# Scattering token rows behind both normalisations of a unit, with one instruction order for every unit of a streamed attention kernel

## The chip, the cores and the metric

The program runs on one core of a Trainium2 chip. The metric is the device time of one execution in microseconds (us), of which the median of several executions is taken. One more execution of the kernel was recorded by the hardware profiler, and all rows below are from that one. PE is TensorE, DVE is VectorE, ACT is ScalarE, POOL is GpSimd and SP is SyncE, which here only issues DMAs.

## The reference, cut to what matters

```
x  = L0_attn_x                                  # 16 x 512 x 256, float32
xn = layernorm(x)
# attention, 16 heads of 64, causal
q, k, v = xn @ Wq, xn @ Wk, xn @ Wv             # per head
wei = softmax(where(causal, q @ k.T * 64**-0.5, -inf))
att = concat_heads(wei @ v) @ Wo + bo
# experts: 16 experts of width 128, two chosen per token by sigmoid(xn @ gate_w + gate_b)
shared = (silu(xn @ swg) * (xn @ swu)) @ swd
routed = sum over the two chosen experts of value * (silu(xn @ wg[e]) * (xn @ wu[e])) @ wd[e]
out = x + att + (xn + shared + routed)
```

## The kernel before, in words

A first stage (some 100 us) normalises the tokens, stores the normalised rows in DRAM, computes the gate values and splits the weights in a high and a low part. Then one long stream runs through 128 **units**. Unit u is one pair of heads of one batch of 512 tokens: batch u // 8, pair u % 8. A **step** of the stream is one turn of the loop `for u in STEPS`, and each engine has its own copy of that loop with its own order of work.

In step u PE does the following, each part with a letter and line of the profile:

- the transposes of unit u's normalised probabilities in three fills, **t3**, **t1** and **t20** (the fill's number names the blocks of 128 query rows that it holds; 16, 8 and 16 transposes, L690);
- the scores of unit u + 1 in three fills, **s3**, **s1** and **s20** (L701);
- the projections k, v and q of unit u + 2 (L663, L676), the output projection of a finished pair (L731, with L736 in two units of a batch), in one unit of a batch the shared gate and up projections (L747), in another the transposes of the next batch's tokens (L758);
- the product of probabilities and v, L715, with which the step ends.

t3, t1 and t20 of unit u wait for POOL. POOL multiplies the exponentials by the inverse sums (`normalise`, L1314) in two groups of four instructions: the **first normalisation** (blocks 3 and 1) and the **second normalisation** (blocks 2 and 0). In step u POOL normalises unit u + 1. The first group waits for the inverse that DVE writes behind its eight row minima (L986, L992), the second for a later inverse. t3 and t1 need the first group, t20 the second.

POOL has other work in the same queue. In steps with u % 8 of 6, 7, 0 and 1 it adds two things to the running sum of a batch between the two normalisations (`prepare`, L1266 and L1268). In steps 12 to 43 it issues the **scatter** (`scatter`, L1277): each batch's normalised rows go to the places of their two experts in a DRAM table, eight indirect DMAs per batch, four per step. In steps 48 to about 88 it issues gathers of expert weights, and from about step 91 gathers of results, two or more per item (L1305), all behind the second normalisation.

In scatter steps two of the four DMAs stand ahead of the second normalisation and two behind it. There the order of PE and DVE also differs from that of the other steps:

```
def turns_first(u):
    return u < FIRST_SCATTER or u > FIRST_SCATTER + 2 * B
```

FIRST_SCATTER is 12 and B is 16, so the function is false for u from 12 to 44, which is 33 units. Where it is true, PE runs t3, t1, t20, s3, s1, s20. Where it is false, PE runs t3, t1, s3, s1, t20, s20, so that t20 comes later. DVE copies half of every transposed fill out of PSUM (`take_probs`, L979) and follows the same choice: t20's copy stands ahead of the first row minima or between them. ACT's order is the same in both cases. PSUM is a ring of eight banks that the function `order` hands out in PE's order.

In odd steps from 15 to 45, DVE also splits one expert's weights (`split_pack`, L1153, both inputs in SBUF) behind the second inverse.

Of the kernel before, what the change touches and what calls it, by code (L numbers as in the profile page):

```python
# [30 lines left out]
B, T, D = 16, 512, 256  # L31
# [23 lines left out]
FIRST_SCATTER = 12  # L55
# [247 lines left out]
def stream(nc, ins, dram, keep, out):  # L303

    with ExitStack() as ctx:
# [106 lines left out]
        SCATTER_AT = {FIRST_SCATTER + n: (n // 2, n % 2) for n in range(2 * B)}  # L412
# [19 lines left out]
        def half(r):  # L432
            return slice(r * DK, (r + 1) * DK)
# [17 lines left out]
                return {}  # L451
            return {kind: n - back for kind, back in (("dn", 2), ("gu", 1), ("xt", 0)) if 0 <= n - back < SLOT_TILES}

        def turns_first(u):

            return u < FIRST_SCATTER or u > FIRST_SCATTER + 2 * B

        def order(u):

            rows_part = ["t20", "t20", "s3", "s3", "s1", "s1"] if turns_first(u) else ["s3", "s3", "s1", "s1", "t20", "t20"]  # L460
            kinds = ["t3", "t3", "t1", "t1", *rows_part, "s20", "s20", 0, "k", "v", "gate", "q",
                     "o", "up", "sum0", "sum1", "rank0", "rank1", "n0", "n1", 1, "w"]
            for n, kind in enumerate(kinds):
                if kind in (0, 1):
                    for each, t in tick(u, kind).items():
                        yield each, 0, t
                elif there(kind, u):
                    yield kind, int(n > 0 and kinds[n - 1] == kind), u
# [27 lines left out]
        with nc.Block() as block:  # L496
# [153 lines left out]
            def _(pe):  # L650
# [30 lines left out]
                def transposes(fill, u):  # L681
                    to = [take(f"t{fill}", u, r) for r in range(2)]
                    pe.wait_ge(norm_done, 8 * u + NTH[PARTS[fill][-1][0], 1] + 1)
                    slots = sum(i + 1 for i, _ in PARTS[fill])
                    for i, at in PARTS[fill]:
                        for h in range(2):
                            for j in range(i + 1):
                                for r in range(2):
                                    off = (h * slots + at + j) * DK
                                    last = pe.transpose(to[r][:, off:off + DK].bitcast(F32R),  # L690
                                                        moved[half(r), i, h, j * P:(j + 1) * P], ident[half(r), half(r)])
                    last.then_inc(t_ready, 1)
# [119 lines left out]
                for u in STEPS:  # L812
                    attends = 0 <= u < UNITS
                    if attends:
                        transposes(3, u)
                        transposes(1, u)
                    if attends and turns_first(u):
                        transposes(20, u)
                    if there("s3", u):
                        scores(3, u)  # L820
                        scores(1, u)
                    if attends and not turns_first(u):
                        transposes(20, u)
                    if there("s20", u):
                        scores(20, u)
                    ticks(u, 0)
                    if there("k", u):
                        project("k", u)
                        project_v(u)
                    if there("gate", u):  # L830
                        expand("gate", u)
                    if there("q", u):
                        project("q", u)
                    if there("o", u):
                        project_out(u)
                    if there("up", u):
                        expand("up", u)
                    if there("sum0", u):
                        count("sum", u)
                    if there("rank0", u):  # L840
                        count("rank", u)
                    if there("n0", u):
                        turn(u)
                    ticks(u, 1)
                    if attends:
                        weigh(u)
# [128 lines left out]
            def _(dve):  # L975
# [216 lines left out]
                for u in STEPS:  # L1192
                    attends, ahead = 0 <= u < UNITS, there("s3", u)
                    if 0 <= u - 1 < UNITS:
                        split_out(u - 1)
                    if attends:
                        take_probs(3, u)
                        take_probs(1, u)
                    if attends and turns_first(u):
                        take_probs(20, u)  # L1200
                    if ahead:
                        maximum(3, 0, u)
                        maximum(3, 1, u)
                    if attends and not turns_first(u):
                        take_probs(20, u)
                    if ahead:
                        maximum(1, 0, u)
                        maximum(1, 1, u)
                        maximum(2, 0, u)
                        maximum(2, 1, u)  # L1210
                        maximum(0, 0, u)
                        maximum(0, 1, u)
                        invert(31, u + 1)
                    route(u, 0)
                    n = tick(u, 0)
                    if "gu" in n:
                        slot_gate(n["gu"])
                        slot_widen(n["gu"])
                    if "xt" in n:
                        split_xt(n["xt"])  # L1220
                    if there("k", u):
                        split_projected("k", u)
                    if "gu" in n:
                        split_slots(n["gu"])
                    if there("v", u) and u % 2:
                        take_v(u)
                    if there("gate", u):
                        gate(u)
                    if there("q", u):
                        split_projected("q", u)  # L1230
                    if ahead:
                        invert(20, u + 1)
                    if there("o", u):
                        add_out(u)
                    if there("up", u):
                        widen(u)
                    if u in PACK_AT:
                        split_pack(PACK_AT[u])
                    if there("n0", u):
                        split_normal(u)  # L1240
                    done = [m for m, item in enumerate(ITEMS) if item[0] == u - 1]
                    n = tick(u, 1)
                    if "gu" in n:
                        slot_gate(n["gu"])
                        slot_widen(n["gu"])
                    if "xt" in n:
                        split_xt(n["xt"])
                    if there("up", u):
                        split_hidden(u)
                    if "gu" in n:  # L1250
                        split_slots(n["gu"])
                    for part in range(2):
                        for m in done:
                            add_routed(m, part)
                    route(u, 1)

            @block.gpsimd
            def _(pool):
# [68 lines left out]
                for u in STEPS:  # L1327
                    b, k = (u + 2) // PAIRS, (u + 2) % PAIRS
                    if there("s3", u):
                        for i in (3, 1):  # L1330
                            for h in range(2):
                                normalise(i, h, u + 1)
                    if 0 <= b < B and k < QT:
                        prepare(b, k)
                    n = TICKS.get((u, 0))
                    if n is not None and 1 <= n and n + 1 < SLOT_TILES:
                        gather_weights(n + 1)
                    if u == FIRST_TICK - 1:
                        for t in range(2):
                            gather_weights(t)  # L1340
                    if u in SCATTER_AT:
                        scatter(*SCATTER_AT[u], 0)
                    if there("s20", u):
                        for i in (2, 0):
                            for h in range(2):
                                normalise(i, h, u + 1)
                    n = TICKS.get((u, 1))
                    if n is not None and 1 <= n and n + 1 < SLOT_TILES:
                        gather_weights(n + 1)
                    if u in SCATTER_AT:  # L1350
                        scatter(*SCATTER_AT[u], 1)
                    for m, item in enumerate(ITEMS):
                        if item[0] == u:
                            gather_rows(m)
# [49 lines left out]
```

## Time and profile before

| | |
|---|---|
| median of 3 executions | 1960.73 us (1960.04 to 1964.51) |
| the profiled execution's own time | 1962.58 us |
| its span from the first to the last instruction | 1960.9 us |
| mean granted TensorE clock | 0.989 of full speed |
| busy: PE, DVE, ACT, POOL | 1892.3, 1406.0, 1218.2, 1020.2 us |
| units 12 to 44 in the trace (first transpose of unit 12 to that of unit 45) | 282.34 to 706.87 us |

The time of an execution is a little longer than its span. A unit is found in the trace by its first transposes, which follow the previous unit's L715. PE's time in a unit can be read as a **head**, from the first transpose to the first matmul behind the scores, and a rest.

### The profile page before, as it was taken

What the parts mean: (1) busy time and instruction counts of PE and PEld (TensorE: products, weight loads), DVE (VectorE), ACT (ScalarE), POOL (GpSimd) and SP (SyncE); (2) the same over time, 40 slices, a digit from 0 to 9 for tenths busy, and PEclk for the clock granted to TensorE, in tenths of its full rate; (3) what the DMA queues carried; (4) which work ended last, traced back from release to release, by engine and by line L of the source; (5) the groups of instructions that cost most, each with busy time, mean ns of one, the idle gap of its engine ahead of it and who ended that gap; (6) DMA issues with size and microseconds to landing.
All of it is one profiled execution on the core that took longest, in us unless ns stands there. A gap on an engine that the chain in (4) does not pass through costs nothing.

```text
span 1960.9 us, 53515 instructions
## 1 busy us (share of the span) xinstructions
PE 1892.3 (97%) x20556; PEld 1748.2 (89%) x20558; DVE 1406.0 (72%) x4086; ACT 1218.2 (62%) x3340; POOL 1020.2 (52%) x1512
## 2 busy tenths in 40 slices
PE   5879999999999999999999999999999999999998
PEld 5868898888889898999999999999999999888897
DVE  7658886767676676666766667667667888878875
ACT  3355566666666565666665666666666666656564
POOL 2133447777776644344343343344344867687742
PEclk9999999999999999999999999999999999999999
DMA  8534422434343312544545445545432232333200
GB/s 246 192 109 175 153 94 82 138 106 146 109 146 109 114 68 71 194 153 148 175 157 178 147 154 167 171 162 173 147 103 77 87 119 87 114 95 120 70 29 12
DMA packets 158603, 249.92 MB, mean 127 GB/s; under 512 B 27280, under 2 KB 112528, under 8 KB 158352
## 3 DMA queue, kind: packets, MB, share of 16 engines
q1 hardware_dynamic: 134688, 150.79, 23.4%
q0 software_dynamic: 23664, 95.70, 14.8%
q8 instruction: 167, 2.74, 0.6%
q14 instruction: 84, 0.69, 0.1%
HBM read 151.54 MB, written 94.90 MB: 126 GB/s over the span
## 4 chain that ended last, share of the span: by engine, by line
PE 65%; POOL 16%; issue 8%; DVE 3%; ACT 3%; DMA 0%; POOLq 0%; SPq 0%; DVEq 0%
PE d_bank L663 13%; PE d_bank L715 10%; POOL d_probs L1314 9%; PE d_bank L701 9%; PE d_bank L690 8%; PE d_bank L731 6%; PE d_bank L676 6%; PE d_bank L789 6%; POOL queued_rows L1277 4%; PE d_bank L776 3%; ACT d_probs L860 2%; PE d_bank L747 2%; DVE d_probs L986 1%; POOL d_rows L1305 1%; PE d_bank L799 1%
## 5 line engine op out<-in xcount | busy, mean ns | idle before, releaser
L1314 POOL TENSOR_SCALAR d_probs<-d_probs,d_inverse 128x512 f32<-128x512 f32 (+3 forms) x1024 | 554.7, 556 | 756.6 <-DVE d_inverse L992 755.3
L860 ACT ACTIVATE d_probs<-d_probs,d_bias 128x512 f32<-128x512 f32 (+3 forms) x1024 | 562.4, 553 | 119.4 <-DVE d_bias L986 119.4
L986 DVE CUSTOM_DVE_ANT_0 d_probs<-d_bank,mask 128x512 f32<-128x512 f32 (+3 forms) x1024 | 432.5, 484 | 3.2 <-PE d_bank L701 2.5
L663 PE MATMUL d_bank<-d_xnt,wqk_all 128*128 128x512 f32 x1536 | 414.0, 405 | 1.5 <-DVE d_xnt L1039 1.5
L663 PEld LDWEIGHTS d_bank<-d_xnt,wqk_all 128*128 128x128 f32 x1536 | 274.6, 191 | 54.9 <-DVE d_xnt L1039 1.7
L715 PE MATMUL d_bank<-d_probs_t,d_v 128*64 128x128 f32 x5120 | 308.9, 276 | 0.0
L701 PE MATMUL d_bank<-d_ks,d_qs 64*128 64x512 f32 (+3 forms) x3072 | 290.5, 332 | 8.3 <-issue 6.9
L715 PEld LDWEIGHTS d_bank<-d_probs_t,d_v 128*64 128x64 f32 x5120 | 278.1, 137 | 17.1 <-issue 5.4
L701 PEld LDWEIGHTS d_bank<-d_ks,d_qs 64*128 64x128 f32 x3072 | 251.8, 191 | 24.3 <-issue 7.7
L690 PEld LDWEIGHTS d_bank<-ident_r,d_probs_moved 64*128 64x128 f32 x5120 | 226.1, 136 | 48.5 <-issue 48.2
L690 PE MATMUL d_bank<-ident_r,d_probs_moved 64*128 64x64 f32 x5120 | 244.1, 245 | 22.8 <-POOL d_probs L1314 22.0
L853 ACT ACTIVATE d_probs_t<-d_bank 128x512 f32<-128x512 f32 (+1 forms) x384 | 188.2, 525 | 102.1 <-PE d_bank L690 91.9
L997 DVE TENSOR_TENSOR d_qs<-d_bank,d_qs 128x512 fp32r<-128x512 f32 x128 | 88.5, 691 | 201.6 <-ACT d_qs L866 201.6
L878 ACT ACTIVATE d_out_t<-d_bank 128x512 fp32r<-128x512 f32 x128 | 76.4, 597 | 249.5 <-PE d_bank L715 249.5
L979 DVE COPY d_probs_t<-d_bank 128x512 f32<-128x512 f32 (+1 forms) x384 | 209.1, 591 | 8.4 <-PE d_bank L690 7.9
L731 PEld LDWEIGHTS d_bank<-wo_all,d_out_t 128*128 128x128 f32 x1536 | 201.1, 190 | 12.2 <-issue 1.7
L676 PEld LDWEIGHTS d_bank<-wv_all,d_xnt 128*128 128x128 f32 x1536 | 199.4, 190 | 11.1
L731 PE MATMUL d_bank<-wo_all,d_out_t 128*128 128x256 f32 x1536 | 206.7, 281 | 1.5 <-DVE d_out_t L1008 1.5
L676 PE MATMUL d_bank<-wv_all,d_xnt 128*128 128x256 f32 x1536 | 201.2, 281 | 0.0
L860 ACT ACTIVATION_READ_ACCUMULATOR d_probs<-d_probs,d_bias 128x1 f32 x1024 | 194.8, 190 | 0.0
L1008 DVE TENSOR_TENSOR d_out_t<-d_bank,d_out_t 128x512 fp32r<-128x512 f32 x128 | 88.2, 689 | 111.6 <-ACT d_out_t L878 110.7
L1305 POOL DMA_INDIRECT d_rows<-routed_rows,slot x128 | 132.1, 1032 | 34.6 <-issue 34.6
(122 smaller groups left out, 2292.6 us busy)
## 6 DMA issues: line engine op xcount, KB each, us to landing
queued_rows<-d_zeros SPq DMA_DIRECT2D x79, 256.0 KB, 2.4
d_x<-queued_rows SPq DMA_DIRECT2D x79, 256.0 KB, 3.4
routed_rows<-d_y SPq DMA_DIRECT2D x79, 256.0 KB, 2.3
expert_rows<-d_w SPq DMA_DIRECT2D x32, 384.0 KB
a_x_in<-in_L_attn_x SPq DMA_DIRECT2D x16, 512.0 KB, 7.5
xn_rows<-a_xn SPq DMA_DIRECT2D x16, 512.0 KB, 5.2
d_normal<-xn_rows SPq DMA_DIRECT2D x32, 256.0 KB, 3.7
d_base<-in_L_attn_x SPq DMA_DIRECT2D x32, 256.0 KB, 2.9
```

The lines of the kernel that those rows point to most:

```text
L663: last = pe.matmul(to[:, :], wqk[:, n % PAIRS, "qk".index(kind), wa, k, :], xnt[n // PAIRS % 2][:, xb, k, :], start=first, stop=(k == KD - ...
L676: last = pe.matmul(to[:, t * 2 * P:(t + 1) * 2 * P], xnt[b % 2][:, xa, k, tok * P:(tok + 1) * P], wv[:, wb, k, cols], start=(k == 0 and (x ...
L690: last = pe.transpose(to[r][:, off:off + DK].bitcast(F32R), moved[half(r), i, h, j * P:(j + 1) * P], ident[half(r), half(r)])
L701: last = pe.matmul(to[h][:, at * P:at * P + cols], qs[r][qa][half(h), i * P:(i + 1) * P], ks[r][kb][half(h), 0:cols], start=(n == 0), stop ...
L715: last = pe.matmul(to[half(h), i * P:(i + 1) * P], v[u // 2 % 2][:, j, col:col + DK], probs_t[fill][:, h, at + j, :], start=(j == 0), stop ...
L731: last = pe.matmul(to[:, s * D:(s + 1) * D], out_t[g % 2][oa][:, j, cols], wo[:, wb, g % 4 * GROUP + j, :], start=(j == 0 and n == 0), sto ...
L853: act.activation(probs_t[fill][:, :, :, half(0)], bank(f"t{fill}", u)[:, 0:2 * slots * DK].rearrange("p (h j n) -> p h j n", h=2, n=DK), A ...
L860: act.activation(part, part, ACT.Exp, bias=bias[:, i, h:h + 1], scale=-1.0, accum_out=total[which][:, at % 4:at % 4 + 1]).then_inc(exp_don ...
L979: dve.tensor_copy(probs_t[fill][:, :, :, half(1)], bank(f"t{fill}", u, 1)[:, 0:2 * slots * DK].rearrange("p (h j n) -> p h j n", h=2, n=DK ...
L986: dve.tensor_tensor_reduce(out=probs[:, i, h, 0:cols], in0=bank(f"s{fill}", u, h)[:, at * P:at * P + cols], in1=mask[:, T - cols:T], scale ...
L1305: pool.indirect_dma_start(out=rows[m % 4 // 2][:, m % 2 * 2 + n, :], out_offset=None, in_=dram["routed"][:, :], in_offset=bass.IndirectOff ...
L1314: pool.tensor_scalar(part, part, inverse[which][:, at % 4:at % 4 + 1], 1.0, ALU.mult, ALU.mult).then_inc(norm_done, 1)
```

## The change

All four scatter DMAs of a step are issued behind the second normalisation, and `turns_first` is gone: every unit takes the order t3, t1, t20, s3, s1, s20 on PE, with DVE's copy of t20 ahead of the row minima. The numbers of instructions and DMAs don't change.

```diff
-        def turns_first(u):
-
-            return u < FIRST_SCATTER or u > FIRST_SCATTER + 2 * B
-
         def order(u):
 
-            rows_part = ["t20", "t20", "s3", "s3", "s1", "s1"] if turns_first(u) else ["s3", "s3", "s1", "s1", "t20", "t20"]
+            rows_part = ["t20", "t20", "s3", "s3", "s1", "s1"]
...
                     if attends:
                         transposes(3, u)
                         transposes(1, u)
-                    if attends and turns_first(u):
+                    if attends:
                         transposes(20, u)
                     if there("s3", u):
                         scores(3, u)
                         scores(1, u)
-                    if attends and not turns_first(u):
-                        transposes(20, u)
                     if there("s20", u):
                         scores(20, u)
...
                     if attends:
                         take_probs(3, u)
                         take_probs(1, u)
-                    if attends and turns_first(u):
+                    if attends:
                         take_probs(20, u)
                     if ahead:
                         maximum(3, 0, u)
                         maximum(3, 1, u)
-                    if attends and not turns_first(u):
-                        take_probs(20, u)
                     if ahead:
                         maximum(1, 0, u)
                         maximum(1, 1, u)
...
-                    if u in SCATTER_AT:
-                        scatter(*SCATTER_AT[u], 0)
                     if there("s20", u):
                         for i in (2, 0):
                             for h in range(2):
...
                     if u in SCATTER_AT:
-                        scatter(*SCATTER_AT[u], 1)
+                        for half_of in range(2):
+                            scatter(*SCATTER_AT[u], half_of)
```

**POOL, the third scatter step (step 14, where `prepare` runs too).** d_base and d_normal are the running sum, d_probs the probabilities, queued_rows the DRAM table. Before:

```order
L1314 TENSOR_SCALAR d_probs<-d_probs,d_inverse 128x512 [waits d_inverse_done] x2
L1314 TENSOR_SCALAR d_probs<-d_probs,d_inverse 128x256 [waits d_inverse_done] x2
L1266 TENSOR_TENSOR d_base<-d_base,d_normal 128x256
L1268 TENSOR_TENSOR d_base<-d_base,d_bo 128x256 [waits d_x_summed]
L1277 DMA queued_rows<-d_rows_994,slot 20224x256 [waits d_rows_loaded1]
L1277 DMA queued_rows<-d_rows_994,slot 20224x256
L1314 TENSOR_SCALAR d_probs<-d_probs,d_inverse 128x384 [waits d_inverse_done] x2
L1314 TENSOR_SCALAR d_probs<-d_probs,d_inverse 128x128 [waits d_inverse_done] x2
L1277 DMA queued_rows<-d_rows_994,slot 20224x256 [waits d_rows_loaded1]
L1277 DMA queued_rows<-d_rows_994,slot 20224x256
```

After:

```order
L1306 TENSOR_SCALAR d_probs<-d_probs,d_inverse 128x512 [waits d_inverse_done] x2
L1306 TENSOR_SCALAR d_probs<-d_probs,d_inverse 128x256 [waits d_inverse_done] x2
L1258 TENSOR_TENSOR d_base<-d_base,d_normal 128x256
L1260 TENSOR_TENSOR d_base<-d_base,d_bo 128x256 [waits d_x_summed]
L1306 TENSOR_SCALAR d_probs<-d_probs,d_inverse 128x384 [waits d_inverse_done] x2
L1306 TENSOR_SCALAR d_probs<-d_probs,d_inverse 128x128 [waits d_inverse_done] x2
L1269 DMA queued_rows<-d_rows_994,slot 20224x256 [waits d_rows_loaded1]
L1269 DMA queued_rows<-d_rows_994,slot 20224x256
L1269 DMA queued_rows<-d_rows_994,slot 20224x256 [waits d_rows_loaded1]
L1269 DMA queued_rows<-d_rows_994,slot 20224x256
```

The second normalisation (the rows with 384 and 128 columns) has moved up past two DMAs, and all four DMAs now stand between it and the first normalisation of the next step.

**PE, the head of unit 13.** The rows with ident_r are transposes, those with d_ks and d_qs scores, d_bank is a PSUM bank. Before:

```order
L690 MATMUL d_bank<-ident_r,d_probs_moved 128x64 [waits d_norm_done,d_p_out,d_s_out]
L690 MATMUL d_bank<-ident_r,d_probs_moved 128x64 x7
L701 MATMUL d_bank<-d_ks,d_qs 128x512 [waits d_p_out,d_v_out0]
L701 MATMUL d_bank<-d_ks,d_qs 128x512 x5
L701 MATMUL d_bank<-d_ks,d_qs 128x256 [waits d_p_out,d_w_out,d_o_out]
L701 MATMUL d_bank<-d_ks,d_qs 128x256 x5
L690 MATMUL d_bank<-ident_r,d_probs_moved 128x64 [waits d_norm_done,d_t_out1,d_t_out0]
L690 MATMUL d_bank<-ident_r,d_probs_moved 128x64 x15
L701 MATMUL d_bank<-d_ks,d_qs 128x384 [waits d_p_out,d_t_out1,d_t_out0]
```

After:

```order
L686 MATMUL d_bank<-ident_r,d_probs_moved 128x64 [waits d_norm_done,d_p_out,d_s_out]
L686 MATMUL d_bank<-ident_r,d_probs_moved 128x64 x7
L686 MATMUL d_bank<-ident_r,d_probs_moved 128x64 [waits d_norm_done,d_p_out,d_v_out0]
L686 MATMUL d_bank<-ident_r,d_probs_moved 128x64 x15
L697 MATMUL d_bank<-d_ks,d_qs 128x512 [waits d_p_out,d_w_out,d_o_out]
L697 MATMUL d_bank<-d_ks,d_qs 128x512 x5
L697 MATMUL d_bank<-d_ks,d_qs 128x256 [waits d_p_out,d_t_out1,d_t_out0]
L697 MATMUL d_bank<-d_ks,d_qs 128x256 x5
L697 MATMUL d_bank<-d_ks,d_qs 128x384 [waits d_p_out,d_t_out1,d_t_out0]
```

t20 (the transposes with x15 behind) has moved up ahead of s3 and s1, and with it the bank that s3 takes: it now waits for DVE's copy of the previous unit's product (d_w_out), which s1 waited for before.

## Rows read from the trace of the kernel before

**Rows 1.** The page, busy time of each engine with its share and its instructions.
```profile
PE 1892.3 (97%) x20556; PEld 1748.2 (89%) x20558; DVE 1406.0 (72%) x4086; ACT 1218.2 (62%) x3340; POOL 1020.2 (52%) x1512
```

**Rows 2.** Busy time by stretch: scatter stage, unit 25, unit 41.
```profile
core 0: us, PE busy (x) PEld busy (x) DVE busy (x) ACT busy (x) POOL busy (x), PEclk, DMA share, GB/s
282.34:706.87 424.53, 417.47 (x4757) 379.35 (x4756) 297.49 (x881) 272.85 (x774) 295.32 (x424) 0.99 0.35 116
...
446.38:461.70 15.32, 14.88 (x154) 13.03 (x152) 11.43 (x30) 9.46 (x25) 12.44 (x18) 1.00 0.35 113
650.20:669.77 19.57, 17.44 (x155) 15.27 (x154) 11.46 (x30) 9.56 (x25) 13.91 (x20) 0.83 0.27 89
```

**Rows 3.** Waits from 282 to 707 us: total, times, longest.
```profile
POOL d_probs L1314 <- DVE d_inverse L992: 95.6, 35, 7.1
...
PE d_bank L690 <- POOL d_probs L1314: 7.1, 12, 2.1
```

**Rows 4.** PE in time, head of unit 29: start, length, work [idle before].
```profile
498.72 1.17 PE L690 MATMUL d_bank<-ident_r,d_probs_moved 64*128 64x64 f32 x24
...
500.88 0.81 PE L690 MATMUL d_bank<-ident_r,d_probs_moved 64*128 64x64 f32 x16
...
502.53 1.66 PE L663 MATMUL d_bank<-d_xnt,wqk_all 128*128 128x512 f32 x6
```

**Rows 5.** PE in time, head of unit 25, which began at 446.38.
```profile
449.12 0.83 PE L690 MATMUL d_bank<-ident_r,d_probs_moved 64*128 64x64 f32 x16 [0.44 <-POOL d_probs L1314]
...
450.79 1.66 PE L663 MATMUL d_bank<-d_xnt,wqk_all 128*128 128x512 f32 x6
```

**Rows 6.** POOL in time, step 24, which normalises unit 25.
```profile
440.82 2.27 POOL L1314 TENSOR_SCALAR d_probs<-d_probs,d_inverse 128x512 f32<-128x512 f32 x4 [1.82 <-DVE d_inverse L992]
...
443.88 0.73 POOL L1268 TENSOR_TENSOR d_base<-d_base,d_bo 128x256 f32<-128x256 f32 x1
444.77 1.07 POOL L1277 DMA_INDIRECT queued_rows<-d_rows,slot  x1 [0.16 <-issue]
...
447.14 1.84 POOL L1314 TENSOR_SCALAR d_probs<-d_probs,d_inverse 128x384 f32<-128x384 f32 x4
```

**Rows 7.** DVE in time: the second inverse of step 24, the weight split of step 45.
```profile
444.56 0.17 DVE L992 RECIPROCAL d_inverse<-d_total 128x4 f32<-128x4 f32 x1
...
717.83 0.95 DVE L1153 TENSOR_TENSOR d_w<-d_raw,d_w 128x768 fp32r<-128x768 f32 x1
```

**Rows 8.** PE in time, head of unit 46, where t20 stands first.
```profile
719.38 1.84 PE L690 MATMUL d_bank<-ident_r,d_probs_moved 64*128 64x64 f32 x40
...
723.10 1.65 PE L663 MATMUL d_bank<-d_xnt,wqk_all 128*128 128x512 f32 x6
```

**Rows 9.** POOL in time, second normalisation of step 45, without scatter.
```profile
716.82 2.54 POOL L1314 TENSOR_SCALAR d_probs<-d_probs,d_inverse 128x384 f32<-128x384 f32 x4 [1.25 <-DVE d_inverse L992]
```

**Rows 10.** POOL in time, step 94 and the beginning of step 95, with gathers.
```profile
1533.07 2.34 POOL L1314 TENSOR_SCALAR d_probs<-d_probs,d_inverse 128x384 f32<-128x384 f32 x4 [0.21 <-DVE d_inverse L992]
...
1541.28 2.26 POOL L1314 TENSOR_SCALAR d_probs<-d_probs,d_inverse 128x512 f32<-128x512 f32 x4 [0.71 <-DVE d_inverse L992]
```

**Rows 11.** PE in time, head of unit 95.
```profile
1534.41 1.98 PE L690 MATMUL d_bank<-ident_r,d_probs_moved 64*128 64x64 f32 x40
...
1538.45 1.65 PE L663 MATMUL d_bank<-d_xnt,wqk_all 128*128 128x512 f32 x6
```

**Rows 12.** POOL in time, step 40: the second of its four DMAs.
```profile
651.66 0.98 POOL L1277 DMA_INDIRECT queued_rows<-d_rows,slot  x1 [2.00 <-issue]
```

**Rows 13.** PE in time, t20 of unit 41.
```profile
654.64 1.20 PE L690 MATMUL d_bank<-ident_r,d_probs_moved 64*128 64x64 f32 x16 [2.13 <-POOL d_probs L1314]
```

**Rows 14.** POOL in time, first normalisation of step 111, behind six gathers of step 110.
```profile
1745.31 2.27 POOL L1314 TENSOR_SCALAR d_probs<-d_probs,d_inverse 128x512 f32<-128x512 f32 x4
```

**Rows 15.** PE in time, t20 of unit 112, which step 111 normalises.
```profile
1751.96 0.83 PE L690 MATMUL d_bank<-ident_r,d_probs_moved 64*128 64x64 f32 x16 [2.18 <-POOL d_probs L1314]
```

## The prediction, made before the changed kernel was run

> **What bounds the kernel now.** I read the page first. PE is busy for 1892.3 us [rows 1] of a span of 1960.9 us, so PE's own program is the bound, and an edit can only give what PE waits or what an order of its work costs. The change touches units 12 to 44, so I then read that stretch: it takes 424.53 us, of which PE is busy for 417.47 [rows 2]. The table of waits of the stretch names what stops it. PE waits 12 times for POOL's normalisation, 7.1 us in all, the longest 2.1 [rows 3]. POOL itself waits 35 times, 95.6 us, for DVE's inverse [rows 3]: POOL has time to spare, only not at the right place. The timeline shows the place.
>
> In unit 29 the head runs without a wait from 498.72 to 502.53, that is 3.81 us, and t20 starts 2.16 us into it [rows 4]. In unit 25 t20 waits 0.44 us [rows 5], and the head takes 450.79 - 446.38 = 4.41 us [rows 2, 5]. Read for every unit, the heads are 3.81 us (3.80 to 3.87) in 21 of the 33, 4.34 to 4.54 in eleven (15 to 17, 23 to 25, 31 to 33, 39, 40; together 48.74 us, and unit 25 is their pattern), and one, unit 41, is far longer. These twelve are the units whose normalisation shares a step with the two additions of `prepare`. In step 24 POOL starts the first normalisation at 440.82, ends the additions at 444.61, and could go on to the second normalisation, since its inverse is written at 444.73 [rows 6, 7]. But the two scatter DMAs run from 444.77, and the second normalisation starts at 447.14 only, and ends at 448.98 [rows 6]. PE's t20 starts 0.14 us later [rows 5]. So the DMAs' place costs PE time in these twelve units, and in no others.
>
> **Term 1, the new order by itself.** Where t20 already stands ahead of the scores, the same head takes 723.10 - 719.38 = 3.72 us [rows 8], against 3.81 [rows 4]. In 21 units without a wait this gives 21 x 0.09 = 1.9 us. The work is the same; only one change of kind between transposes and scores less is to be seen. Bound from below: nothing, if the 0.09 belongs to something else of that stretch.
>
> **Term 2, eleven short stalls.** The second normalisation can now start when inverse and additions are done: 444.75 in the pattern unit, ending at 444.75 + 1.84 = 446.59, 0.2 us behind the first transpose of unit 25 at 446.38 instead of 2.6 behind. t20 is also wanted earlier, behind t3 and t1 and no longer behind s3 and s1. How late is too late shows in unit 95, where this order is already run: the normalisation ends at 1535.41 [rows 10], 1.00 us behind the first transpose at 1534.41, and the head is 4.04 us, 0.32 over 3.72 [rows 8, 11]. So up to 0.68 us behind costs nothing, and 0.2 is inside. The eleven heads fall to 3.72: 48.74 - 11 x 3.72 = 7.8 us. The lower bound is 11 x 0.09 = 1.0 us, if t20 waits as long as before in its new place; the upper bound is what I take.
>
> **Term 3, unit 41.** It takes 19.57 us against the 15.32 of unit 25, which does the same work [rows 2]. Here POOL stood still for 2.00 us ahead of the second DMA of the step, where 0.30 is usual [rows 12]; PE then waited 2.13 us [rows 13], and the granted clock fell to a mean of 0.83 in this unit [rows 2], so part of it ran at 1.2 GHz instead of 2.4. Among the 128 scatter DMas it is the only pause of this kind. What causes it the trace does not show. If it belongs to this DMA, the 114th that POOL issues, it will lie behind the second normalisation, where POOL waits for DVE anyway. Then unit 41 comes down to unit 25's time and by term 2's 0.7 us: 19.57 - 15.32 + 0.70 = 4.95 us. If it belongs to a place in POOL's instructions it hits the second normalisation itself: that ended 2.4 us late by DMAs, and now 1.7 us late by the pause, so about half the wait stays, and perhaps the low clock. Bounds 0 and 5; I take the whole, since an idle queue makes a pause in the middle of DMAs the likelier.
>
> **Term 4, a charge.** In odd steps DVE splits weights, for 0.95 us [rows 7], right behind the second inverse. Until now a scatter DMA lay beside it; now the second normalisation does. In step 45, where that is so already, the normalisation takes 2.54 us against 1.84 [rows 6, 9]: 0.70 us longer. In most odd steps it is done long before t20. Units 16, 24, 32 and 40 (steps 15, 23, 31, 39) have both additions and split: 0.2 + 0.70 = 0.9 us behind, and with the start scattering by 0.1 this is 0.2 to 0.3 over the 0.68. Charge: 4 x 0.3 = 1.2 us. Steps 17, 25, 33 and 41 have both too, but contain the shared projections, which keep PE in the unit some 3 us longer.
> The Trainium skill ("SBUF — State Buffer", on the shared port of GpSimd and VectorE) says that a VectorE instruction with both inputs in SBUF and a GpSimd instruction that reads SBUF shut each other out for a whole instruction. The stretch of step 45 agrees (0.70 of 0.95 us). By the rule taken strictly the full 0.95 would be lost.
>
> **What lies behind the DMAs now.** Four indirect DMAs in a row take from 1535.41 to 1541.28 - 0.71 = 1540.57, that is 5.2 us, and POOL then still waits 0.71 us for the next inverse [rows 10]. In a scatter step they would end at 446.6 + 5.2 = 451.8; the next first normalisation began at 453.3 and will be wanted 0.7 us earlier with a shorter unit, at 452.6. That cover is 0.8 us. Beyond it there is more: the first normalisation ended at 443.09, 3.3 us ahead of t3 [rows 2, 6], but a late one pushes the additions and the second normalisation, which have 0.5 us only. SP waits for the last scatter of a batch before it loads the next rows; these land some 1.8 us later. The loads behind it have most of a unit until someone needs them, so I cost this at nothing; without that cover it would be 1.8 us in each of 14 batches, 25 us. DVE's copy of t20 moves ahead of the row minima, with the same instructions in all, and ACT keeps its order. Unit 46 runs so without a wait [rows 8].
>
> **Sum.** 1.9 + 7.8 + 4.95 - 1.2 = 13.5 us. Some units of the stretch also have a rest 0.05 to 0.09 us longer than like units elsewhere, about 1 us in all; I count half. Gain 14.0 us. On the profiled execution: span 1960.9 to 1946.9, time 1962.6 to 1948.6. The median lies 1.85 us below that execution's time, so 1960.7 - 14.0 = **1946.7 us**.
>
> **Rivals.**
> A, the forecast: 1946.7, its own range 1943 to 1950. Chance 0.60.
> B, the pause or a stall like it stays, or shows in another place, and takes back term 3: 1946.7 + 5.0 = 1951.7. For it: units with heads over 5 us exist elsewhere without scatter (unit 112 [rows 15]), and their cause need not be where the DMA is. Against it: the one pause lies at a DMA. Chance 0.14.
> C, the two second bounds hold together: t20 waits in its new place as before, as it is wanted 1.3 us earlier, and only term 1 and a part of the pause remain: 1960.7 - 2.9 - 1 = 1956.8, not to be told from no change. Against it: unit 95's threshold. Chance 0.10.
> D, by the port: second normalisation and weight split exclude each other whole, 0.25 us more in the four units of term 4, and the split in its turn is late and holds DVE's next copy by as much: 1946.7 + 4 x 0.5 = 1948.7. This is what the Trainium skill's page named above would make of it. Chance 0.10.
> E, slower: the block of DMAs becomes the thing that PE waits for. In step 110 six DMAs stand in a row, the next first normalisation starts with no wait at all [rows 14], and t20 of unit 112 waits 2.18 us [rows 15]. If four scatter DMAs took what six gathers take, 2.6 us more, twelve heads would be 3.72 + 2.5 = 6.2 instead of 4.4: + 21 us, less term 1's 1.9, so 1980. It decides from a block 1.5 us longer than 5.2. Two scatter DMAs take 447.14 - 444.77 = 2.37 us [rows 6], two gathers 5.2 / 2 = 2.6 [rows 10], so little speaks for it. Chance 0.06.
>
> **Chances and range.** A difference of 0.3% (5.9 us, a time below 1954.8 or above 1966.6) is about what a measurement of this kernel can tell from no change. A, B and D are faster by more, a little of B not: 0.83. C and that part: 0.11. E: 0.06. The range from 1942 to 1955 holds nearly all of A, B and D and leaves out C and E.
>
> **What would show it.** Right: no PE wait for POOL over 0.4 us in units 12 to 44, heads of 3.72 there, 4.0 in units 16, 24, 32 and 40; POOL's second normalisation starting 0.1 us behind the inverse or the additions; the stretch at 409 to 411 us instead of 424.5; the pause of 1.7 us at a DMA behind the second normalisation. Wrong: first normalisations that start with no wait for the inverse; t20 waiting in its new place; a low clock in another unit; a longer stretch outside units 12 to 44.

## The result, and the profile after

The changed kernel takes 1943.9 us (median of 6 executions, 1942.7 to 1949.1) against 1960.2 for the kernel before (median of 6 beside it). The ratio is 0.9924 with a 95% interval of 0.9905 to 0.9942, a difference clear of the noise: some 15 us faster, where 14.0 were forecast and 1946.7 us named. The profiled execution has a span of 1943.9 us against 1960.9.

The page of the changed kernel, busy times as in [rows 1], and the engines' shares of the chain that ended last, changed kernel first and the kernel before under it:

```profile
PE 1885.9 (97%) x20558; PEld 1744.8 (90%) x20558; DVE 1402.0 (72%) x4086; ACT 1222.1 (63%) x3340; POOL 1021.0 (53%) x1512
...
PE 85%; POOL 4%; DVE 2%; issue 2%; ACT 1%; DMA 0%; POOLq 0%; SPq 0%; DVEq 0%
...
PE 65%; POOL 16%; issue 8%; DVE 3%; ACT 3%; DMA 0%; POOLq 0%; SPq 0%; DVEq 0%
```

POOL does as much work as before, and its share of the chain fell from 16% to 4%. Then the same stretches as in [rows 2], found by the same first transposes: units 12 to 44, unit 25, unit 41, and one unit outside, 120 (columns as there):

```profile
280.22:689.49 409.27, 409.27 (x4756) 374.58 (x4755) 293.06 (x881) 276.61 (x774) 296.67 (x424) 1.00 0.37 121
439.88:454.41 14.53, 14.53 (x154) 12.91 (x152) 11.20 (x30) 9.58 (x25) 11.41 (x17) 1.00 0.32 101
638.26:652.79 14.53, 14.53 (x155) 12.90 (x154) 11.19 (x30) 9.58 (x25) 11.43 (x17) 1.00 0.31 102
1838.39:1855.06 16.67, 14.48 (x142) 13.17 (x141) 11.88 (x32) 8.09 (x23) 10.95 (x17) 0.80 0.16 49
```

PE is busy for the whole 409.27 us, 15.26 less than before, and the table of waits of the stretch no longer has one of PE for POOL. The other 1.7 us of the span lie outside the stretch, where both kernels do the same work: the units ahead of 12 took 2.1 us less, the end behind unit 127's first transpose 1.3 less, and units 45 to 126 took 1.7 more, with unit 120 at a mean clock of 0.80. That unit took 14.13 us before and takes 16.67 now, with the same wait for POOL of 2.2 us in both; in the changed kernel the clock fell behind the wait, in the kernel before it stayed at 1.00. The five kernels of experiments 1 to 5 leave this unit as it is, and it takes 15.66, 15.67, 15.59, 14.09 and 15.58 us there. So a whole time moves by 2 to 3 us for reasons outside the change, and from now on I compare the stretch.

PE at the head of unit 25, which answers [rows 5], and POOL in the two steps ahead of it:

```profile
439.88 1.84 PE L686 MATMUL d_bank<-ident_r,d_probs_moved 64*128 64x64 f32 x40
441.55 2.12 PE L697 MATMUL d_bank<-d_ks,d_qs 64*128 64x512 f32 x24
443.61 1.65 PE L659 MATMUL d_bank<-d_xnt,wqk_all 128*128 128x512 f32 x6
```

```profile
426.42 2.54 POOL L1306 TENSOR_SCALAR d_probs<-d_probs,d_inverse 128x384 f32<-128x384 f32 x4
429.12 1.07 POOL L1269 DMA_INDIRECT queued_rows<-d_rows,slot  x1 [0.17 <-issue]
...
433.04 0.98 POOL L1269 DMA_INDIRECT queued_rows<-d_rows,slot  x1 [0.30 <-issue]
434.44 2.28 POOL L1306 TENSOR_SCALAR d_probs<-d_probs,d_inverse 128x512 f32<-128x512 f32 x4 [0.41 <-DVE d_inverse L986]
...
437.50 0.73 POOL L1260 TENSOR_TENSOR d_base<-d_base,d_bo 128x256 f32<-128x256 f32 x1
438.43 1.84 POOL L1306 TENSOR_SCALAR d_probs<-d_probs,d_inverse 128x384 f32<-128x384 f32 x4 [0.20 <-DVE d_inverse L986]
```

The head is 3.73 us, as was 4.41. The second normalisation of step 24 ends at 440.27, 0.4 us behind the first transpose (2.6 before). That of step 23 takes 2.54 us, as it lies beside DVE's weight split:

```profile
425.90 0.17 DVE L986 RECIPROCAL d_inverse<-d_total 128x4 f32<-128x4 f32 x1
...
426.56 1.24 DVE L1147 TENSOR_TENSOR d_w<-d_raw,d_w 128x768 fp32r<-128x768 f32 x1
```

The split itself takes 1.24 us here against 0.95 [rows 7]. The normalisation ends at 428.96, 0.96 us behind unit 24's first transpose at 428.00, and the head of unit 24 is 3.82 instead of 3.72.

And POOL in step 40, where it paused:

```profile
638.80 1.07 POOL L1269 DMA_INDIRECT queued_rows<-d_rows,slot  x1 [0.16 <-issue]
640.74 0.98 POOL L1269 DMA_INDIRECT queued_rows<-d_rows,slot  x1 [0.87 <-issue]
...
644.70 2.28 POOL L1306 TENSOR_SCALAR d_probs<-d_probs,d_inverse 128x512 f32<-128x512 f32 x4 [0.42 <-DVE d_inverse L986]
```

The pause is at the same DMA, the 114th, behind the normalisation now, and it is 0.87 us instead of 2.00, where 0.30 is usual. POOL still waits 0.42 us for DVE after the block, and unit 41 is a plain 14.53 us.

### The profile page after: what moved, and what is told of

It reads as the page before. It is cut to its first block, busy times and chain, and to the rows that moved or that the text cites. A ratio compares the mean times of both kernels' runs of the same rounds, so it can differ in the third digit from the quotient of the medians.

```text
span 1943.9 us, 53517 instructions
## 1 busy us (share of the span) xinstructions
PE 1885.9 (97%) x20558; PEld 1744.8 (90%) x20558; DVE 1402.0 (72%) x4086; ACT 1222.1 (63%) x3340; POOL 1021.0 (53%) x1512
## 4 chain that ended last, share of the span: by engine, by line
PE 85%; POOL 4%; DVE 2%; issue 2%; ACT 1%; DMA 0%; POOLq 0%; SPq 0%; DVEq 0%
PE d_bank L659 18%; PE d_bank L711 14%; PE d_bank L697 12%; PE d_bank L686 10%; PE d_bank L727 9%; PE d_bank L672 8%; PE d_bank L785 6%; PE d_bank L772 3%; POOL d_probs L1306 3%; PE d_bank L743 2%; POOL d_rows L1297 1%; PE d_bank L795 1%; DVE d_probs L980 1%; PE d_bank L732 1%; PE d_bank L754 1%
## 5 line engine op out<-in xcount | busy, mean ns | idle before, releaser
L697 PE MATMUL d_bank<-d_ks,d_qs 64*128 64x512 f32 (+3 forms) x3072 | 283.4, 331 | 8.3 <-issue 6.9
L686 PE MATMUL d_bank<-ident_r,d_probs_moved 64*128 64x64 f32 x5120 | 239.1, 245 | 14.0 <-POOL d_probs L1306 13.5
```

The costliest lines, as they stand in the source:

```text
L686: last = pe.transpose(to[r][:, off:off + DK].bitcast(F32R), moved[half(r), i, h, j * P:(j + 1) * P], ident[half(r), half(r)])
L697: last = pe.matmul(to[h][:, at * P:at * P + cols], qs[r][qa][half(h), i * P:(i + 1) * P], ks[r][kb][half(h), 0:cols], start=(n == 0), stop ...
```

## The experiments

**1. The scatter's move alone.** All four DMAs behind the second normalisation; PE's and DVE's order of before.

```diff
-                    if u in SCATTER_AT:
-                        scatter(*SCATTER_AT[u], 0)
                     if there("s20", u):
...
                     if u in SCATTER_AT:
-                        scatter(*SCATTER_AT[u], 1)
+                        for half_of in range(2):
+                            scatter(*SCATTER_AT[u], half_of)
```

> The scatter's move alone: all four DMAs behind the second normalisation, PE and DVE in the order of before. Theory (the DMAs' place made t20 wait, and the order is worth 0.09 us a unit on top): no wait of PE for POOL in units 12 to 44, all 33 heads at 3.81 us, also in units 16, 24, 32 and 40, since t20 is wanted 1.3 us later there; the stretch of units 12 to 44 takes 412 to 413 us (409.3 in the changed kernel, 424.5 in before), the time is about 1947, some 3 us over the changed kernel. Rival (the gain comes from the common order of PE, which takes t20's PSUM banks and DVE's copies out of the middle of the scores): most of the stretch's 15 us stays, 420 us or more.

1950.0 us (1946.6 to 1951.0), ratio to before 0.9947 (0.9934 to 0.9961). The stretch of units 12 to 44, and the head of unit 25:

```profile
280.99:693.79 412.80, 412.80 (x4756) 377.16 (x4754) 294.21 (x881) 272.76 (x774) 296.79 (x424) 1.00 0.36 120
```

```profile
441.93 1.17 PE L690 MATMUL d_bank<-ident_r,d_probs_moved 64*128 64x64 f32 x24
...
444.08 0.82 PE L690 MATMUL d_bank<-ident_r,d_probs_moved 64*128 64x64 f32 x16
...
445.73 1.66 PE L663 MATMUL d_bank<-d_xnt,wqk_all 128*128 128x512 f32 x6
```

Every wait is gone and every head is 3.80 or 3.81 (12: 3.88), in units 16, 24, 32 and 40 too. This part gives 424.53 - 412.80 = 11.7 of the 15.3 us. The time was expected at about 1947 and is 1950.0, 6.1 us over the changed kernel's. Of the 4.5 us by which the spans of the two profiled executions differ the stretch holds 3.5. PE is busy without a gap in the stretch in this kernel and in the changed one, so the 3.5 us that the order adds are PE's own work running faster: 0.09 us in each head (2.4 us in all, after the 0.45 that four heads lose with the order), and 0.05 to 0.09 in some rests (1.1 us).

**2. The order alone.** t20 ahead of the scores everywhere; two DMAs stay ahead of the second normalisation.

```diff
                    if attends:
                        transposes(3, u)
                        transposes(1, u)
-                    if attends and turns_first(u):
+                    if attends:
                        transposes(20, u)
...
-                    if attends and not turns_first(u):
-                        transposes(20, u)
```

(with DVE's copy and the PSUM ring in the same order)

> The order alone: t20 ahead of the scores in all units, but two scatter DMAs still ahead of the second normalisation. Theory: t20 is wanted 1.3 us earlier while the normalisation ends as late as before, so the heads of the twelve units behind a step with additions grow from 4.4 to about 5.6 us, units behind an odd step with a weight split get some 0.4 us, the others fall to 3.72. That is 15 us more than before, and up to 40 if waits near 2 us bring the clock down as in unit 41: 1975 us, between 1970 and 2000. Rival (both parts help by themselves): 3 us less than before, 1957.

1976.1 us (1974.3 to 1979.9), ratio 1.0091 (1.0076 to 1.0106): slower. The stretch takes 440.34 us, 15.8 more than before. Unit 25 begins at 451.22 and its head is 5.48 us:

```profile
453.98 0.83 PE L686 MATMUL d_bank<-ident_r,d_probs_moved 64*128 64x64 f32 x16 [1.59 <-POOL d_probs L1306]
...
456.70 1.65 PE L659 MATMUL d_bank<-d_xnt,wqk_all 128*128 128x512 f32 x6
```

So the two parts do not add: the order is worth 3.5 us behind the move and costs 15.8 without it. Twelve units, those whose normalisation ends early enough, have heads of 3.72 or 3.73 here too. Eight units have the wait of 1.59 or 1.60 us: in six of them the head is 5.47 to 5.49, in units 17 and 32 it is 6.94 and 7.48, as the granted clock fell behind the wait (0.50 of full speed from 545.5 to 550.4). In unit 41 POOL's pause, once more of 2.00 us and once more at the 114th DMA, came on top, and t20 waited 3.30 us.

**3 and 4. A fifth and a sixth DMA in each scatter step.** The changed kernel, with one or two more indirect DMAs behind the four; they write rows to a table that nobody reads, so nothing is left out.

```diff
-                        for n in range(2):
+                        for n, to in ((0, "queued"), (1, "queued"), (0, "spare"), (1, "spare"))[:2 + EXTRA * half_of]:
...
-                                out=dram["queued"][:, :],
+                                out=dram[to][:, :],
```

(EXTRA is 1 or 2, and the counts that are waited for grow with it)

> The changed kernel with a fifth indirect DMA in each scatter step, which writes rows once more to a table that nobody reads. The block behind the second normalisation grows by 1.3 us to 6.5. POOL's wait for the inverse behind the block was 0.4 to 1.0 us in steps with additions, so it is used up, and the second normalisation of the next such step ends 0.4 to 0.9 us later. Theory (cover of 0.4 to 0.9 us, then each microsecond counts in these units alone): 3 us more than the changed kernel, between 1 and 7. Rival (the first normalisation has 3 us of cover, so a longer block costs nothing): no difference.

> As with five, but six DMAs in each scatter step, 7.8 us. Theory: first normalisations start 1.7 to 2.2 us late, t20 waits 1.3 to 2 us in the eight to twelve units behind steps with additions, none elsewhere, since there POOL waits 1.7 us for the second inverse: 10 to 20 us more than the changed kernel, more if the clock falls. Rival: no difference. In both kernels with more DMAs the pause of POOL at DMA 114 moves to an earlier step (34 with five a step, 30 with six) if it belongs to the count of DMAs, and stays in step 40 if it belongs to the place in the program.

Five: 1948.4 us (1945.1 to 1953.4), ratio to before 0.9948 (0.9930 to 0.9967), stretch 411.82 us, 2.6 more than with four. Four heads (16, 24, 32, 40) are 4.27 to 4.29 and four (17, 25, 33, 41) 3.91 to 3.93; together 2.6 us, all other units are as with four. Six: 1962.7 us (1958.4 to 1968.1), ratio 1.0019 (1.0007 to 1.0030), stretch 427.94, 18.7 more than with four and 3.4 more than in the kernel before. POOL in step 23 and PE at unit 24, which begins at 432.11:

```profile
427.84 0.97 POOL L1270 DMA_INDIRECT spare_rows<-d_rows,slot  x1 [0.30 <-issue]
428.82 2.27 POOL L1307 TENSOR_SCALAR d_probs<-d_probs,d_inverse 128x512 f32<-128x512 f32 x4
431.07 1.48 POOL L1259 TENSOR_TENSOR d_base<-d_base,d_normal 128x256 f32<-128x256 f32 x1
```

```profile
435.31 0.83 PE L687 MATMUL d_bank<-ident_r,d_probs_moved 64*128 64x64 f32 x16 [2.03 <-POOL d_probs L1307]
435.96 3.70 PE L698 MATMUL d_bank<-d_ks,d_qs 64*128 64x512 f32 x24
```

The first normalisation begins with no wait, t20 waits 2.03 us, and the scores behind it take 3.70 us against 2.12, as the clock fell (0.52 of full speed from 435.96 to 439.50): that head is 7.48 us. It happens once in eight units (16, 24, 32 and 40, heads 7.42 to 7.93), while units 23, 31 and 39 lose 0.6 us, and units 17, 25, 33 and 41, each behind one of the long ones, lose nothing. The pause of POOL was at neither expected place: with five DMAs 0.94 us at a weight gather at 1297.63, with six 1.69 us at 1015.47.

**5. The weight splits one step earlier.** In even steps instead of odd ones.

```diff
-        PACK_AT = {FIRST_SCATTER + 3 + 2 * e: e for e in range(E)}
+        PACK_AT = {FIRST_SCATTER + 2 + 2 * e: e for e in range(E)}
```

> The changed kernel with DVE's weight splits one step earlier, in the even steps 14 to 44, so that they lie beside the second normalisation in steps with additions 14, 16, 22, 24, 30, 32, 38 and 40 instead of 15, 23, 31 and 39. Theory (the 0.1 us that the heads of units 16, 24, 32 and 40 have over 3.72 comes from the split beside the normalisation): these four fall to 3.72, units 15, 23, 31, 39 (behind steps with u % 8 of 6) and 17, 25, 33, 41 (behind 0) rise to between 3.8 and 4.2, and the time stays within 3 us of the changed kernel. Rival (the 0.1 us comes from POOL's late start behind the four DMAs): units 16, 24, 32 and 40 keep 3.83.

1949.0 us (1946.4 to 1950.0), ratio 0.9941 (0.9925 to 0.9958), stretch 412.84, 3.6 us more. Units 16, 24, 32 and 40 fell to 3.72 or 3.73. Units 15, 23, 31, 39 and 17, 25, 33, 41 rose to 4.05 to 4.07, and so did 19, 27, 35 and 43, which I had not named: their step has no additions. 12 x 0.33 - 4 x 0.11 = 3.5 us. POOL and PE around unit 25, which begins at 440.26:

```profile
438.91 2.54 POOL L1306 TENSOR_SCALAR d_probs<-d_probs,d_inverse 128x384 f32<-128x384 f32 x4 [0.20 <-DVE d_inverse L986]
```

```profile
441.60 0.84 PE L686 MATMUL d_bank<-ident_r,d_probs_moved 64*128 64x64 f32 x16 [0.17 <-POOL d_probs L1306]
```

The same 2.54 us as in step 23 above, now ending 1.19 us behind the first transpose. In even steps the normalisation starts later, since ACT takes v between the exponentials there and DVE writes the second inverse later (438.65, 1.61 us ahead of the first transpose, against 425.90, 2.10 ahead, in step 23). The cause of the charge is shown: it goes where the split goes. The split itself takes 1.00 us beside this normalisation, hardly more than its 0.95.

**6. The other indirect DMAs in the same way.** The weight gathers of step 48 go behind the second normalisation, and no step issues more than four result gathers (six in steps 110 to 113 and 118 before). These are two edits in one run; unit 49 belongs to the first, the units from 112 on to the second.

```diff
-            for _ in range(2):
+            for _ in range(2 - sum(item[0] == u for item in ITEMS)):
                 if waiting and u >= waiting[0][0] * PAIRS + 12:
...
-                    if u == FIRST_TICK - 1:
-                        for t in range(2):
-                            gather_weights(t)
                     if there("s20", u):
                         for i in (2, 0):
                             for h in range(2):
                                 normalise(i, h, u + 1)
+                    if u == FIRST_TICK - 1:
+                        for t in range(2):
+                            gather_weights(t)
```

> The same idea for the other indirect DMAs: the two weight gathers of step 48 stand behind the second normalisation too, and no step issues more than four result gathers (before, steps 110 to 113 and 118 to 121 had up to six). Theory: t20 of unit 49 no longer waits 1.86 us, that of unit 112 not 2.2 us, and the clock has no reason to fall in either; unit 49 loses 3 to 5 us of its 22.3, units 112 to 115 together about 6 of 59, unit 120 up to 4, so that the time is 1932 to 1939 against 1943.9. Rival (the delayed gathers are wanted later by the end of the program, or the slots' loads bound unit 49): same time as the changed kernel or slower, with new waits behind unit 122.

1934.5 us (1932.8 to 1935.4), ratio to before 0.9871 (0.9855 to 0.9888). Units 112 to 115 took 52.0 us together instead of 59.0, and unit 120 12.06 instead of 16.67. Unit 49 gave back 1.15 us only: in the changed kernel it had waited 1.86 us for POOL and 1.16 for the load of the scattered rows; now the first wait was gone and the second was 2.93.

```profile
743.01 0.57 PE L795 MATMUL d_bank<-ident_r,d_x 128*128 128x128 f32 x4 [2.93 <-DMA d_x<-queued_rows]
743.38 2.89 PE L659 MATMUL d_bank<-d_xnt,wqk_all 128*128 128x512 f32 x6
```

**7. And the first load of rows a unit earlier.**

```diff
+                        if u == FIRST_TICK - 1 and slot == 3:
+                            load_slots(0)
                         n = TICKS.get((u, slot // 2))
                         if n is not None and slot % 2:
-                            if n == 0:
-                                load_slots(0)
```

> The kernel with all gathers behind too, and the first load of scattered rows issued in step 48 instead of 49. Theory (in unit 49 PE waited 2.9 us for this load once POOL's normalisation was no longer late, and the clock fell after it): the wait is gone, the clock stays up, and unit 49 falls from 21.1 us to between 16.5 and 17.5, so that the time is 1929 to 1932 against 1934.5. Rival (something else holds PE there too, such as the row load behind other queue work or the first use of the weights in the same unit): unit 49 stays over 19 us and the time within 1.5 us.

1929.8 us (1925.8 to 1932.0), ratio 0.9847 (0.9834 to 0.9861), the fastest version. Unit 49 in this kernel:

```profile
737.55:754.15 16.60, 16.60 (x174) 15.17 (x172) 12.39 (x34) 10.44 (x28) 9.26 (x15) 1.00 0.45 153
```

16.60 us with PE busy throughout, against 22.28 in the changed kernel and 21.13 in experiment 6; there it had waited 2.93 us, and the rest of the 4.5 us was the low clock (2.89 us for six matmuls in the second row above, which take 1.62 here).

## Why the prediction was right, and where its sizes were off

**Term 1 (the order, 1.9 us over 21 units).** Right: the 21 heads lost 1.9 us. Between experiment 1 and the changed kernel the order is worth 3.5 us over all 33 units, 2.9 in the heads before the charge of term 4, and 1.1 in the rests. It does not need the move in every unit: in experiment 2 twelve heads are at 3.72 or 3.73 without it. But the stretch as a whole gains by the order only behind the move, since the other units lose more. Why one change of kind less saves 0.09 us the runs do not tell.

**Term 2 (eleven stalls, 7.8 us).** Right. The heads fell to 3.72 except for the charge. (The additions of `prepare` share a step with the normalisation of 16 units, not only of the twelve that waited; units 18, 26, 34 and 42 follow a longer unit and had no wait.) Experiment 1 shows that the move alone ends the waits, experiment 2 that t20's earlier need is real. The mechanism of rival C, t20 waiting in its new place, is what happens with the order alone.

What was wrong is the threshold of 0.68 us, read from unit 95. The 24 transposes of t3 and t1 take 1.00 us (446.38 to 447.38 in unit 25 of the kernel before), and t20 starts 0.14 us behind the end of the normalisation [rows 5, 6], so a normalisation that ends up to 0.86 us behind the first transpose should cost nothing, and what comes later should cost its full length. The heads of four kernels say the same: 0.10 us lost at 0.96 behind (changed kernel, unit 24), 0.33 at 1.19 (experiment 5), 0.57 at 1.42 (experiment 4, unit 23), 1.76 at 2.62 (experiment 2, unit 25). In unit 95 something else came last. DVE was adding up expert results (d_acc), so it copied the product of unit 94 out of its PSUM bank late, and s3, which takes that bank, began 0.09 us behind the copy (rows of the kernel before):

```profile
1533.46 2.22 DVE L1189 SCALAR_TENSOR_TENSOR d_acc<-d_rows,weight,d_acc 128x256 f32<-128x256 f32 x4
1535.61 0.68 DVE L1008 TENSOR_TENSOR d_out_t<-d_bank,d_out_t 128x512 fp32r<-128x512 f32 x1
```

```profile
1536.38 2.14 PE L701 MATMUL d_bank<-d_ks,d_qs 64*128 64x512 f32 x24
```

By the threshold of 0.86 the normalisation accounts for 0.14 of its 0.32 us, and this copy for the rest. In units 24 and 25 of the changed kernel the same copy ends 0.3 and 0.2 us ahead of s3.

**Term 3 (unit 41, 4.95 us).** Right in size: 19.57 to 14.53 us is 5.04. The step that the whole of it comes back rested on the pause staying at its DMA, and it did here, in experiments 1, 2, 6 and 7. But it is not a matter of the count: experiments 3 and 4 had it at other DMAs and experiment 5 had none of its size in the scatter. Neither of the two readings of term 3 survives, and the cause stays open, so that the pause stayed where the forecast wanted it was luck in part. Its size also differs: 2.00 us in the two kernels with two DMAs ahead of the second normalisation, 0.87 in the four that have all behind it and show the pause in the scatter. The term did not need the smaller size: with 2.00 us the block of step 40 would end 1.13 us later, and the first normalisation of unit 42, which waits 0.42 us there, would start 0.71 us later, 7.4 instead of 8.09 us ahead of its unit (an estimate); in experiment 3 it starts 7.31 us ahead, and unit 42 loses nothing.

**Term 4 (the charge, 1.2 us).** Right mechanism, too large. The four heads lost 0.13, 0.10, 0.11 and 0.11 us, 0.45 in all. The normalisation was stretched by the 0.70 us of the row, to 2.54, and it ended 0.96 us behind the first transpose, where the forecast had 0.9 to 1.0. What was set too low was the threshold: 0.86 and not 0.68, as under term 2. Experiment 5 shows both the cause and the slope, 1.19 us behind costing 0.33.
The Trainium skill ("SBUF — State Buffer", section "SBUF: two separate sides") says that whichever of the two instructions starts first has the port for its whole length and the other is blocked (rival D). The traces agree that they hold each other up, but not with a loss of the whole 0.95 us: in units 16, 24, 32 and 40 POOL lost 0.70 us and DVE 0.29 to 0.31. In the changed kernel's eight other splits beside a normalisation POOL lost the same 0.70, and DVE 0.04 or nothing. How the loss is shared the runs do not explain. The 0.25 us a unit more that D asked for did not come.

**The cover behind the DMAs.** The text gave 0.8 us; POOL waits 0.41 us behind the blocks of steps 23, 39 and 40, and 0.9 to 1.0 behind those of steps 22 and 24. The fifth DMA of 1.3 us took it up and cost 0.45 us in four units and 0.2 in four, so the later covers counted as well. Rival E, that the block becomes what PE waits for, is a real mechanism: a block 1.3 us longer costs 2.6 us, one 2.6 us longer costs 18.7 and with it the whole gain. It reaches 1962.7 us instead of 1980, since one unit in eight pays most of it, not twelve in 33. Rival B was not seen in the stretch; of its kind is the low clock of unit 120 outside it, which the prediction had named as a sign of being wrong and which took back 2.5 us, with the same wait of PE as before and in a unit that the change does not touch. SP's later landings cost nothing that could be found: PE has no gap in the stretch.

**The sum.** 409 to 411 us for the stretch, measured 409.27; 14.0 us forecast, 15.3 measured in the stretch and some 15 in the time. Term by term the stretch gave 1.9 + 7.8 + 5.04 - 0.45, and 1.0 in the rests, of which the forecast had counted half. The charge and the rests make up nearly all of the 1.3 us by which the forecast was small.

## What to carry to other kernels

In an in-order queue, ask of each DMA issue not what it costs but what stands behind it: two issues of 1.3 us in each step cost 11.7 us in all (4.9 of them in unit 41, where the pause came on top) ahead of a normalisation that PE waits for, and nothing behind it. An order that wants its input earlier may be tried only after the input has been made earlier; alone, it showed the opposite sign. When a wait is removed, look up what PE waits for next at that place before counting the gain, and count a wait of 2 us on PE as up to two and a half times its length, for the clock (unit 32 of experiment 4 waits 2.03 us and is 5.1 us longer). A threshold that is read from one row holds only if nothing else was waited for in that row.

## What the runs showed of the hardware that was not expected

Waits of PE of 1.6 to 2.2 us cost more than themselves in some places and not in others. Behind 2.19 us in unit 120 the changed kernel ran the next scores at 1.2 GHz (16.67 us); the kernel before, behind 2.18 us in the same unit, did not (14.13). Within one execution, that of experiment 2, eight units wait 1.59 or 1.60 us, and the clock falls behind two of these waits. VectorE's two-input subtraction of the weight split and GpSimd's scaling hold each other up: side by side GpSimd lost 0.70 us every time in the changed kernel, and VectorE 0.29 to 0.31 where it began 0.14 us behind the scaling, 0.04 or nothing where it began 0.4 or 1.0 us behind. A scatter DMA that began 0.13 us behind the start of a split took 1.75 or 1.76 us instead of 1.07 (four times in the changed kernel). Back-to-back indirect DMAs of 128 rows follow each other on GpSimd at 1.27 to 1.4 us. In eight of the nine profiled executions one of them comes 0.6 to 1.7 us late; the runs show where it fell, but not why.
